# Grouping TensorE's work of a scan and attention stage by tile form

## What is computed

```
S = C @ B.T                          # 128 x 128 in a chunk, upper part masked
y = (S * decay) @ (dt * x) + D * x + C @ h * decay0
h = h * decay1 + B.T @ (dt * x * decay2)
attn = softmax(causal(q @ k.T)) @ v
```

## Time and profile before

| what | value |
|---|---|
| median of 3 runs | 864.25 us (862.42 to 871.44) |
| the profiled execution's own time | 864.34 us |
| its span | 862.6 us |
| TensorE busy (matmuls) | 788.2 us, 91% |
| VectorE busy | 610.4 us, 71% |
| ScalarE busy | 502.4 us, 58% |
| GpSimd busy | 318.7 us, 37% |
| granted TensorE clock, mean | 0.993 of full speed |

### The profile page before, as it was taken

The page is one execution under the profiler, slowest core; times in us unless marked ns, Lnnn a source line. Parts: engine busy times, 40 slices in busy tenths (PEclk is TensorE's granted clock), DMA queues, the critical chain, the costliest instruction groups (busy, mean ns, idle before and its releaser), DMA issues. The chain is left out here.

```text
span 862.6 us, 18148 instructions
## 1 busy us (share of the span) xinstructions
PE 788.2 (91%) x5472; PEld 483.5 (56%) x5472; DVE 610.4 (71%) x1467; ACT 502.4 (58%) x960; POOL 318.7 (37%) x600
## 2 busy tenths in 40 slices
PE   2779999999999989999999999999999998999897
PEld 1455564756556555655647565475556556475555
DVE  2786479784888758785697848877587866968534
ACT  2435784467753776457844677537765577446652
POOL 5424534053512617045340534226260362505400
PEclk9998999999999999999999999999999999999999
DMA  4000000000000000000000000001000000000000
GB/s 166 2 8 14 14 2 1 9 16 25 0 8 12 26 0 0 8 13 25 0 0 8 14 24 0 2 14 30 1 0 8 12 26 0 0 8 14 25 1 13
DMA packets 15145, 11.73 MB, mean 14 GB/s; under 512 B 1040, under 2 KB 13968, under 8 KB 14992
## 3 DMA queue, kind: packets, MB, share of 16 engines
q1 hardware_dynamic: 15120, 11.43, 4.4%
HBM read 7.76 MB, written 2.10 MB: 11 GB/s over the span
## 5 line engine op out<-in xcount | busy, mean ns | idle before, releaser
L1099 ACT ACTIVATE sb_pr<-S 128x768 f32<-128x768 f32 (+1 forms) x192 | 165.9, 891 | 129.7 <-PE S L444 129.7
L1196 DVE TENSOR_REDUCE sb_mx<-S 128x2 f32<-128x256 f32 (+3 forms) x256 | 198.0, 817 | 29.7 <-PE S L444 29.3
L1716 POOL TENSOR_SCALAR_AFFINE_SELECT sb_pr<-sb_pr 128x256 f32<-128x256 f32 (+1 forms) x192 | 98.9, 517 | 322.2 <-ACT sb_pr L1099 319.7
L444 PE MATMUL R<-sb_pr,sb_va 128*32 128x512 f32 (+3 forms) x1024 | 89.5, 444 | 0.0
L444 PE MATMUL R<-sb_W,sb_pr 128*128 128x96 f32 (+1 forms) x512 | 69.5, 276 | 0.0
L444 PE MATMUL R<-sb_xfT,sb_W 128*128 128x512 f32 x144 | 69.2, 602 | 0.0
L444 PE MATMUL S<-sb_kT,sb_qT 32*128 32x256 f32 (+3 forms) x512 | 56.3, 384 | 13.7 <-DVE sb_mx L1196 10.0
L444 PEld LDWEIGHTS R<-sb_W,sb_pr 128*128 128x128 f32 x512 | 63.5, 192 | 3.8 <-issue 3.5
L444 PEld LDWEIGHTS S<-sb_kT,sb_qT 32*128 32x128 f32 x512 | 27.5, 183 | 66.3 <-DVE sb_mx L1196 58.6
L444 PE MATMUL S<-sb_qT,sb_kT 32*128 32x256 f32 (+3 forms) x512 | 56.3, 384 | 5.7 <-ACT sb_pr L1099 4.9
L1430 DVE SCALAR_TENSOR_TENSOR sb_x<-R,sb_wts,sb_x 128x96 f32<-128x96 f32 x128 | 40.6, 317 | 22.8 <-PE R L444 19.4
(11 more groups left out here) (216 smaller groups left out, 1735.6 us busy)
## 6 DMA issues: line engine op xcount, KB each, us to landing
sb_xin<-x SPq DMA_DIRECT2D x9, 256.0 KB, 2.7
sb_W<-weights SPq DMA_DIRECT2D x1, 2290.0 KB, 11.0
sb_qT<-sb_mT SPq DMA_DIRECT2D x128, 4.0 KB
sb_xres<-x SPq DMA_DIRECT2D x8, 256.0 KB, 2.8
out<-sb_xres SPq DMA_DIRECT2D x7, 256.0 KB, 2.3
sb_cT<-sb_xact SPq DMA_DIRECT2D x8, 128.0 KB, 2.3
sb_W<-weights SPq DMA_DIRECT2D x1, 514.0 KB, 5.8
sb_cst<-consts SPq DMA_DIRECT2D x1, 328.0 KB, 3.1
```

Of the source, the lines that this page charges most:

```text
L444: return pe.matmul(o, lhsT, rhs, start=start, stop=stop, skip_group_check=True)
L1099: act.activation(pr[:, e % 4, :, 0:n], S[pair_of_exp(e)][:, :, 0:n], ACT.Exp).then_inc(p_sb, 1)
L1196: o = dve.tensor_reduce(mx[:, n // P - 1, g, heads[0]:heads[1] + 1], found[:, :, at_col:at_col + n], AX.X, ALU.max, negate=True)
L1716: pool.affine_select(out=keep, in_=keep, compare_op=ALU.is_ge, fill=0.0, base=0, pattern=pattern, channel_multiplier=-1)\
```

## The change

In the second stage TensorE's steps of groups 1 to 3 are put in another order. Each scores step is now followed directly by value products (those of the pair before), and these by one run of full-array work. Three times in a group this gives: scores, values, then

- u 0: `turn_y`, in group 1 `turn_maxima`, `segments`;
- u 2: `turn_values`, `scan_inputs`;
- u 4: `scan_outputs`, then `new_state` (`prep_a` in group 3).

Group 0 keeps its order. `turn_maxima` writes to `R[3]` instead of `R[1]`, so `turn_values` of group 0 waits for its copy. The wait for `wm` now stands inside `scan_outputs`, behind the diagonal products. On ScalarE the copy of the value sums comes one unit earlier, that of `yT` one later, `es` two later, the square of `yz` four later, the copies after `prep_a` two later. On VectorE `values` comes a unit earlier, `scan_products` and `scan_weights` a unit later (from group 1 on), and the tables move the small jobs. On GpSimd `xw` comes a unit later.

```diff
-SIGMOID_AT = {5: (0, 1, 2), 9: (3, 4)}
-JOIN_AT = {11: (0, 1), 15: (2,)}
+SIGMOID_AT = {5: (0, 1, 2), 11: (3, 4)}
+JOIN_AT = {15: (0, 1), 17: (2,)}
...
-STATS_AT = 8
+STATS_AT = 9
...
             def turn_maxima(r, pair, o):
...
-                    pe.wait_ge(seg_sb, at(seg_sb, r, 2))
+                    pe.wait_ge(yz_sb, at(yz_sb, r, 1))
...
             def turn_values(r, g):
...
+                if g == 0:
+                    pe.wait_ge(mT_sb, at(mT_sb, r, 2))
...
             def scan_outputs(r, c):
...
-                pe.wait_ge(wm_sb, at(wm_sb, r, c + 1))
...
                 for n in range(2):
                     mm(R[3][:, n * P:(n + 1) * P], xact[:, n, s], diag_d[:, n, :], c == 0 and n == 0, False)
+                pe.wait_ge(wm_sb, at(wm_sb, r, c + 1))
...
             def new_state(r, c):
...
-                if c == 1:
-                    pe.wait_ge(mT_sb, at(mT_sb, r, 2))
...
-                    if u == 0 and g > 0:
-                        turn_y(r, g - 1)
-                    if u == 1 and g > 0:
-                        weigh_values(r, e - 3)
-                        segments(r, g)
-                        scan_inputs(r, g)
                     if e == 2:
                         segments(r, 0)
-                    if u == 3:
-                        weigh_values(r, e - 3)
-                        if g >= 1:
-                            turn_values(r, g - 1)
+                    if u == 0 and g > 0:
+                        weigh_values(r, e - 2)
+                        turn_y(r, g - 1)
+                        if g == 1:
+                            turn_maxima(r, 1, R[3])
+                        segments(r, g)
+                    if g == 0 and u == 3:
+                        weigh_values(r, 0)
+                    if u == 2 and g > 0:
+                        weigh_values(r, e - 2)
+                        turn_values(r, g - 1)
+                        scan_inputs(r, g)
                     if u == 4:
+                        if g > 0:
+                            weigh_values(r, e - 2)
                         scan_outputs(r, g)
-                    if u == 5:
-                        if g < T - 1:
+                        if g == T - 1:
+                            prep_a(r)
+                        elif g > 0:
                             new_state(r, g)
-                        weigh_values(r, e - 3)
-                    if (g, u) == (1, 2):
-                        turn_maxima(r, 1, R[1])
-                    if (g, u) == (3, 3):
-                        prep_a(r)
+                    if g == 0 and u == 5:
+                        new_state(r, 0)
+                        weigh_values(r, 2)
                 turn_y(r, T - 1)
                 weigh_values(r, G * UNITS - 2)
...
                     if u == 0 and g > 0:
+                        evac_values(r, g - 1)
+                    if u == 1 and g > 0:
                         evac_y(r, g - 1)
-                    if u == 1 and g > 0:
-                        evac_values(r, g - 1)
-                    if u == (2 if g == 0 else 1):
+                        if g == 1:
+                            evac_maxima(r, 1, R[3])
+                    if u == (2 if g == 0 else 3):
                         act.wait_ge(seg_ps, at(seg_ps, r, g + 1))
...
-                    if u == 1 and g > 0:
+                    if u == 5 and g > 0:
                         square_y(r, g - 1)
-                    if (g, u) == (1, 2):
-                        evac_maxima(r, 1, R[1])
...
-                    if (g, u) == (3, 3):
+                    if (g, u) == (3, 5):
                         evac_a(r)
...
-                    if u == 1:
+                    if u == 2 and g >= 1:
+                        values(r, g - 1, ot_ps, ao_sb)
+                    if u == (2 if g else 1):
                         scan_products(r, g)
-                    if u == 2:
+                    if u == (3 if g else 2):
                         scan_weights(r, g)
-                    if u == 3 and g >= 1:
-                        values(r, g - 1, ot_ps, ao_sb)
...
-                    if u == 2 and g < T - 1:
+                    if u == (3 if g else 2) and g < T - 1:
                         pool.wait_ge(xdt_sb, at(xdt_sb, r, g + 1))
```

## The result

| | before | after |
|---|---|---|
| median of 20 runs, us | 864.17 | 870.52 |
| profiled execution (its span), us | 864.34 (862.60) | 871.19 (869.4) |
| first round: groups 1, 2, 3, us | 10.32, 9.50, 10.82 | 9.40, 9.40, 11.49 |
| the seven later rounds, us | 10.26, 9.49, 10.82 | 9.40, 9.40, 12.50 |

The ratio of after to before is 1.0055 [1.0035, 1.0074]. That is within the 1% of the forecast "no change", but the kernel is clearly slower, not equal, and the median lies at the upper end of the predicted range (870.5). One of the 20 runs of after, at 4139 us, was disturbed and is left out of every comparison; the others lie between 868.64 and 871.64, with a median of 870.37, so the two medians lie on either side of that end.

The account below looks back on a forecast made before the run. It took the second stage to be bound by TensorE's work plus a few waits. Groups 2, 1 and 3 gave -0.05 - 0.72 + 0.75 = -0.02 us a round, x 8 = -0.2, so 864.1 us; range 857.5 to 870.5.

Parts of the forecast that it names:

- no change: Whole kernel: forecast of 864.1 us, own range 860 to 868, chance 0.80.
- Group 2, -0.05: Second stage, group 2: old exponential wait of 0.54 gone, new waits come; 9.45 us against 9.50 before.
- predicted wait of 0.31: Group 2, before the 384-column scores: TensorE waits 0.31 us for the second exponential, which ends at 2.99.
- rival one: Groups 2 and 3: second exponential not held up by the value sums' copy, 0.47 less each; 856.6 us; chance 0.10.
- Group 1, -0.72: Second stage, group 1: turn_maxima fills the new wait, old waits of 0.49 and 0.29 go; 9.54 us against 10.26.
- Change from scores to values, 0.10: TensorE, scores to values: the tile form change costs 0.10 us, with 0.00 and 0.21 as its ends.
- Group 3 and the end, +0.75: Group 3 to stage one: only prep_a fills the wait for yz, so 11.56 us against 10.81 before.
- Edits at nothing: Moved ScalarE and VectorE jobs, joins included, and the later store of out cost nothing, each hidden by TensorE's run.
- The prediction's own sign of being wrong: New trace: a value run waiting for its mask by more than 0.3 us would show the forecast wrong.
- Rival two: GpSimd's last two masks late once xw is 0.73 later than reckoned; at 1.46, 875.0 us; chance 0.08.

Follow-up runs that it names:

- joins_last_copy: Changed kernel with join products at unit 21, sum at 23, and the value sums' copy behind the second exponential; ratio 0.9922 against the kernel before.
- joins_last_both: As joins_last_copy, plus group 3's 384-column values put behind scan_outputs and prep_a; ratio 0.9918 against the kernel before.
- joins_end: Changed kernel with all three join parts moved to unit 23, behind yz; median 862.14 us, ratio 0.9944 against the kernel before.

## Why the prediction was right and wrong

**Group 2, -0.05, predicted 9.45:** right, 9.40. The 384-column scores came at 3.04, as predicted to the hundredth, and the 512-column values at 3.61 (3.62). They waited for the second exponential, which the copy of the value sums held up. That this copy was the cause is shown by `joins_last_copy`: taking it away gave 0.45 in group 2 (the rival had reckoned 0.47). Of the predicted wait of 0.31 only 0.20 is recorded as idle. That is no later work: `segments` started at 1.70, but its row of 1.13 us holds the tail of the last matmul and ends at 2.83, where the prediction reckoned from start to start (2.73). In group 3 the copy was worth only 0.10: the scores come 0.22 to 0.28 earlier, but the 512-column values then wait for their mask (0.32 in a later round of `joins_last_both`). So rival one's "0.47 in both groups" would have been too high.

**Group 1, -0.72, predicted 9.54:** right in kind, 9.40. The 384-column scores started at 3.03 (181.81 - 178.78), where the exponential lets them, not at 3.29, because `turn_maxima` and its changes of form cost less than I had taken: it starts 0.27 behind `turn_y`, and `segments` 0.44 behind it. TensorE's timeline of the kernel after, group 1:

```profile
180.00 0.44 PE L626 MATMUL R<-sb_cst,sb_yz 128*128 128x128 f32 x2
180.27 0.60 PE L504 MATMUL R<-sb_cst,sb_mhl 128*16 128x128 f32 x4
180.71 1.02 PE L444 MATMUL R<-sb_rs,sb_cst 128*128 128x512 f32 x2
181.81 0.45 PE L444 MATMUL S<-sb_qT,sb_kT 32*128 32x384 f32 x4
```

**Change from scores to values, 0.10:** too high. Values start 0.43 after a 512-column scores run and 0.38 after the 256-column one. The prediction's prices for these runs, taken where the full array follows, were already 0.44 and 0.38, so nothing comes on top of them, and the lower end of the bound, 0.00, was right. The 0.42 from the 384-column scores to the values is not among the stated prices (0.44); the difference is 0.02.

**Group 3 and the end, +0.75, predicted 11.56:** right for the first round (11.49) and for all rounds of `joins_end` (11.48): the mechanism named, `yz` late and only `prep_a` in its wait, is there with its 0.99. Rearranging this end gave back 0.35. In the seven other rounds group 3 took 12.50, and this is the whole miss: `scan_outputs` at 7.92 instead of 6.96, the end at 12.50 instead of 11.56.

**The step that failed** is in "Edits at nothing": "statistics, reciprocals and joins later on VectorE (done by 4.1 of the next group, before `values` at 5.3)". I gave each its own length and asked only whether VectorE's next customer would be kept waiting. I did not ask what runs on GpSimd at the same time. The joins met `rs` and two masks; the masks were ready at 10.51 (198.69 - 188.18) in the place of the 9.26 reckoned; the values wanted them at 9.83. From there it went on: values 0.66 late, copy of the value sums and second exponential late, `hst` wait 0.31, 512-column values 0.42. The prediction's own sign of being wrong, a value run that waits for its mask by more than 0.3, is there twice. The 0.94 us in seven rounds is 6.6 us; the terms that came out smaller than priced (0.05 and 0.14 in groups 2 and 1) give back 1.5 of it, and group 3 of the first round, shorter than predicted, 0.1.

**Rival two** had named the right place, the masks of the last two units, and a price of that order, for the wrong cause: it laid the delay on `xw`, which started at 6.36 (predicted 6.4). It also set the margin at 0.73 with `rs` at 1.03; with `rs` at 1.49 beside `wm` the margin in the first round is 0.2 (masks ready at 9.61). The line to have read was in the trace of before: the sum of the join took 1.07 us beside `xw` and a mask, with a mean of 973 ns, and the first product, of the same size, 674.

## What to carry to other kernels

Before a VectorE operation with two SBUF inputs is moved, lay its new place over GpSimd's timeline, and price the meeting on both engines: each may have to wait for the whole of the other's instruction, and the short ones suffer most for their length. Instances of one form with different durations in the trace (here 973 against 674 ns) are the sign that such meetings occur. A table of small jobs that was free in one order has to be placed anew when the order changes; here that alone decided between 0.6% slower and 0.6% faster (0.3% by the rounds).

## What the runs showed of the hardware that was not expected

- Meetings run as a chain of turns: join 1.52, `rs` 1.49, join 0.93 and two masks 2.13 us, against 0.67, 1.03, 0.69 and 1.22 alone. Four-column steps of GpSimd went from 0.20 to 0.63 and 0.72 beside a 0.7 us product on VectorE.
- A VectorE operation of 0.94 us with one input of 128 columns in the same place left the masks at 1.22, and operations with one input in PSUM left them at 1.23.
- One input is not always free: beside L1236 of the kernel after (128 columns of one tensor and scalars, on VectorE) a mask of 256 columns took 0.50 instead of 0.41 us (at 201.29).
- Not every change of tile form costs the 0.10 us that the rows of before showed at the values' edges: from scores to values nothing was found beyond the price of scores before the full array, and none from the full array into and out of `turn_maxima` (0.27 and 0.44 us from start to start).
